# Two steps moved in the first attention stage of a decoder block: a weight copy on ScalarE, and the splitting of the next weights on GpSimd

## The chip, the core and the metric

The kernel runs on one core of one Trainium2 chip. Its engines each work through a queue of their own and meet only at semaphores: PE (TensorE, matmuls), DVE (VectorE), ACT (ScalarE), POOL (GpSimd) and SP (SyncE, which issues the DMAs). The metric is the device time of one execution in microseconds (us), and of several executions the median.

## The reference

The program is one decoder layer on 16 sequences of 128 tokens, model width 256, in float32. It has three parts, one after the other, each behind a layer norm and added to `x`:

```
x = x + attn(layernorm(x))            # stage A: windowed differential attention
x = x + xattn(layernorm(x), ctx_512)  # stage B: cross attention
x = x + ffn(layernorm(x))             # stage C: 16 experts, top 6, and a shared one
```

The change touches stage A alone. What it computes, for 16 query heads and 4 key heads of width 128:

```
q, k, v = x @ Wq, x @ Wk, x @ Wv ; q, k = rope(q), rope(k)
a1 = softmax(mask(q[:64] @ k[:64].T / 8)) ; a2 = softmax(mask(q[64:] @ k[64:].T / 8))
diff = relu(a1 - lam * a2) ; diff = diff / (sum(diff) + 1e-6)
out = (diff @ v) @ Wo
```

## The kernel before, in words

Stage A runs over 4 groups `g` of 4 query heads and, in each, over 16 units `u`, one for each sequence. `n = 16 g + u` counts them through. Units stand in chunks `c` of four; `j` is the place in the chunk. The work is pipelined over units. In unit `u` PE computes the scores of sequence `u`, transposes the normed weights of `u-2`, multiplies them by the values, and applies `Wo` to the output of `u-3`. Between these, in up to three slots for each unit, PE projects the q, k and v of the chunk that comes next: `A_SLOT` says which of the six items (k, q0, q1, q2, v, q3) stands in which slot.

The other engines serve this order:
- DVE (L1034 on) takes projections out of PSUM (`qab`, `ktmp`), computes `rec`, `ratio` and `rho` from the sums of the two softmaxes, the difference `a1 - lam a2` (L1072), the row maxima (L1126, L1127), the divisor `rden` (L1083), and adds `Wo`'s result to `x_sb` (L1088).
- ACT takes the transposes out of PSUM (`pt`), applies relu (L1478) and the exponentials (L1434, eight in a unit), copies the attention output (`oah`), and writes the mask into PSUM ahead of the next scores. ScalarE's copies all have line L1401.
- POOL multiplies the difference by `rden` (`a_norm`, L1665). PE's transposes in the same unit (L661, L663) wait for that, by `a_dn`. POOL also adds the two halves of the rotated key (`a_keys`, L1659).

Products are made exact enough by splitting operands into a high part (rounded to fp32r) and a low part (what the rounding left). For the weights of the next group, ACT makes the high part `wah` of a tile (`a_high`), once the tile's present content has been used for the last time, in units 8 to 11; POOL then makes the low part `wal` (`a_low`, L1653), which waits for `a_hi`. There are five such tiles for each group. For `Wo` ACT makes `woh` once in each group, in unit 3, DVE makes `wol` from it (L1131), and PE's `Wo` matmuls of unit 3 (L679) wait for `wol`.

Each engine's order is the order in which its function `a_unit` emits instructions, written out by hand. An engine that waits lets nothing behind it pass, PE's weight loads apart. Where loops over groups run (groups 1 and 2), the order is the same as in group 0.

Of the kernel before, what the change touches and what calls it, by code (L numbers as in the profile page):

```python
# [18 lines left out]
CB = 4  # L19
NC = B // CB  # L20
CW = CB * S
H, HG = 16, 4
# [77 lines left out]
def wait(eng, sem, value):  # L100

    if isinstance(value, int) and value <= 0:
        return
    eng.wait_ge(sem, value)


def decoder_kernel(nc, x, ctx_in, in_wqk, in_wv, in_wo, in_lam, in_taba, in_rawb, in_tabb, in_kvtab,
# [5 lines left out]
    def sem(name):  # L113
        return ctx.enter_context(nc.semaphore(name))

    def sb(stack, name, shape, dt=f32):
        return stack.enter_context(nc.sbuf_tensor(name, shape, dt))

    with ctx:
# [17 lines left out]
        wo = raw_w[:, 0:H * DM].rearrange("p (h d) -> p h d", d=DM)  # L137
# [23 lines left out]
        woh = sb(am, "woh", [128, HG, DM], f32r)  # L161
# [64 lines left out]
        def bank(n):  # L226
            return ps[:, n, :]

        def quads(ap):
            return ap.rearrange("p (h k) -> p h k", k=S)  # L230
# [12 lines left out]
        a_wvl, a_wld = sem("a_wv_loaded"), sem("a_weights_loaded")  # L243
# [10 lines left out]
        a_woh, a_wol, a_ol = sem("a_wo_high"), sem("a_wo_low"), sem("a_o_low")  # L254
        a_o, a_wo, a_y, a_nl = sem("a_o_high"), sem("a_out"), sem("a_x_added"), sem("a_nlam_ready")
# [29 lines left out]
        AN, AV = len(A_ITEMS), A_ITEMS.index("v")  # L285
        A_SLOT = {(0, 1): 0, (1, 0): 1, (1, 1): 2, (2, 1): 3, (3, 0): 4, (3, 1): 5}
# [13 lines left out]
        def a_part(first, final, drain):  # L300
            return "first" if first else "final" if final else "drain" if drain else ""

        def a_tile(item):

            return item - (item > AV)
# [8 lines left out]
        def a_split_tile(w, tile):  # L314
            return w[:, :, 128 * tile:128 * (tile + 1)].rearrange("p k (r n) -> p k r n", r=2)
# [82 lines left out]
        def a_blocks(ap):  # L398
            return [early(ap)[..., p, :] for p in range(XP)] + [late(ap)[..., p, :] for p in range(XP)]

        def by_head(ap):
            return ap.rearrange("p h (b q) -> p b h q", b=2)

        def by_block(ap):
            return ap.rearrange("p (b h q) -> p b h q", b=2, q=QH)
# [993 lines left out]
        def _(act):  # L1399
            def copy(dst, src):  # L1400
                return act.activation(dst, src, ACT.Copy)  # L1401

            def ln_take(m, kt, bk):

                tok = slice(CW * (m % NC), CW * (m % NC + 1))
                act.wait_ge(ln_tp, 2 * m + kt + 1)
                copy(xnf[:, kt, tok], bank(bk)).then_inc(ln_f, 1)
                copy(xnh[:, kt, tok], bank(bk)).then_inc(ln_h, 1)
# [7 lines left out]
            def a_high(g_to, tile):  # L1416

                act.wait_ge(a_raw, g_to * 16 + 16)
                copy(a_split_tile(wah, tile), a_raw_tile(tile)).then_inc(a_hi, 1)

            def a_take_v(g_to, c, turns=1):
                act.wait_ge(a_pj, (g_to * NC + c) * AN + (AV + 1))
                copy(quads(kva[:, c % 2, 2, :]), quads(bank(PJ - AV % turns))).then_inc(a_vf, 1)
# [14 lines left out]
            def a_unit(g, u, first=False, final=False, drain=False):  # L1438
                n, c, j = g * UN + u, u // CB, u % CB

                def slot(s):
                    item = A_SLOT.get((j, s))
                    if item is None or drain or (final and c == NC - 1):
                        pass
                    elif item == AV:
                        a_take_v(g + 1 if c == NC - 1 else g, (c + 1) % NC)
                    elif c == NC - 2 and not final:
                        act.wait_ge(a_pj, (g * NC + (NC - 1)) * AN + (item + 1))
                        a_high(g + 1, a_tile(item))
                    for what in A_EXTRA.get((a_part(first, final, drain), u, s), []):  # L1450
                        if what[0] == "ln":
                            ln_take(what[1], what[2], PJ)
                        elif what[0] == "prep":
                            b_take(0, 0, what, what[1], None, bank(PJ))
                        elif what[0] == "kt2":
                            r = what[1]
                            act.wait_ge(b_kvp, r + 1)
                            if r == 0:
                                act.wait_ge(a_sc, NG * UN - CB)
                            copy(kt2[:, CB * r:CB * (r + 1), :], quads(bank(PJ))).then_inc(b_kvc, 1)  # L1460
                if u == 3 and not drain:
                    if first:
                        act.wait_ge(a_wld, 32)
                    wait(act, a_wo, n - 3)
                    copy(woh[:, :, :], wo[:, bass.ds(g * HG, HG), :]).then_inc(a_woh, 1)
                slot(0)
                two = not (first and u < 2) and not (drain and u >= 2)
                if two:
                    act.wait_ge(a_tp, n - 1)
                    wait(act, a_pv, n - 3)  # L1470
                    copy(pt[:, u % 2, :, :], quads(bank(PTB))).then_inc(a_pt, 1)
                if not (first and u < 1) and not (drain and u >= 1):

                    act.wait_ge(a_df, n)
                    par = (u - 1) % 2
                    wait(act, a_dd, n - 2)
                    for h, e in enumerate(a_blocks(ea[:, par, 0, :])):
                        last = act.activation(e, e, ACT.Relu, accum_out=rsum[:, par, h:h + 1])  # L1478
                    last.then_inc(a_re, 1)
                if not drain:  # L1480
                    exps(n, u, 2, a_mx, a_ex, a_tp, lambda m, h: a_blocks(ea[:, u % 2, m, :])[h])
                slot(1)
                if two:
                    act.wait_ge(a_pv, n - 1)
                    wait(act, a_wo, n - 3)
                    copy(by_head(oah[:, (u - 2) % 2, :, :]), by_block(bank(OB))).then_inc(a_o, 1)
                if not drain and not (final and u >= UN - 2):
                    act.wait_ge(a_ex, n + 1)
                    copy(A_S[u % 2][:, :, 0:SW], maskb[:, :].unsqueeze(1).broadcast_to([128, 2, SW])).then_inc(a_mk, 1)
                if first and u == 1:  # L1490
                    for kt in range(KT):
                        ln_take(2, kt, OB + kt)
                slot(2)
# [74 lines left out]
            for u in range(UN):  # L1568
                a_unit(0, u, first=True)
# [62 lines left out]
        def _(pool):  # L1632
# [18 lines left out]
            def a_low(g_to, tile):  # L1651
                pool.wait_ge(a_hi, g_to * AW + (tile + 1))
                pool.tensor_tensor(a_split_tile(wal, tile), a_raw_tile(tile), a_split_tile(wah, tile).bitcast(f32),  # L1653
                                   ALU.subtract).then_inc(a_lo, 1)
# [20 lines left out]
            def a_unit(g, u, first=False, final=False, drain=False):  # L1675
                n, c, j = g * UN + u, u // CB, u % CB
                if not (first and u < 2):
                    a_norm(n - 2, u % 2)
                if first and u == 2:
                    ln_low(2)  # L1680
                if first and u == 7:
                    ln_low(3)
                if final and u == 8:
                    ln_rstd(4)
                if final and u == 12:
                    ln_low(4)
                if final and u == 13:
                    ln_rstd(5)
                if final and u == 15:
                    ln_low(5)  # L1690
                if drain and u == 0:
                    ln_rstd(6)
                if drain:
                    return
                if final and c >= NC - 2:
                    if u == UN - 2 * CB:
                        a_keys(g, NC - 1)
                    return
                if j == 0:
                    a_keys(g + 1 if c == NC - 1 else g, (c + 1) % NC)  # L1700
                if 0 < u - CB * (NC - 2) <= CB:
                    for s in range(2):
                        item = A_SLOT.get(((u - 1) % CB, s), AV)
                        if item != AV:
                            a_low(g + 1, a_tile(item))

            def c_low(g_to, t):
                pool.wait_ge(c_hi, g_to * TG + (t + 1))
# [59 lines left out]
            for u in range(UN + 1):  # L1768
                n = (NG - 1) * UN + u - 1
# [35 lines left out]
            for g in range(1, CG):  # L1805
                for k in range(NC * TG):
                    c, t = k // TG, k % TG
# [122 lines left out]
```

## Time and profile before

| | |
|---|---|
| median of 3 runs | 1346.95 us (1345.06 to 1347.26) |
| the profiled execution's own time | 1345.06 us |
| its span, first to last instruction | 1343.3 us |
| PE busy | 94% of the span |
| mean granted TensorE clock | 0.993 of full speed |

The span is what the engines worked in; 1.8 us of the execution lie around it. PE means matmuls, PEld their weight loads, which overlap them. A row of a timeline gives start, duration, engine, line, operation, output and inputs; `x2` behind it says that two like instructions were merged, and the square bracket says how long the engine had been idle and whose event ended that. Instructions of one engine overlap by about 0.1 us, since the next starts while the last writes its end.

### The profile page before, as it was taken

The numbers are of one execution on the slowest core, as the hardware profiler recorded it, in microseconds if no ns is written. First come the engines' busy times: TensorE is split into PE (matmuls) and PEld (weight loads), VectorE is DVE, ScalarE is ACT, GpSimd is POOL, SyncE is SP. The second block draws the span as 40 slices with busy tenths as digits, with TensorE's granted clock in tenths as the row PEclk, the third lists the DMA queues.
The fourth block names the chain that finished last, engine by engine and source line by source line (L and its number), as shares of the span: only waits on it lengthen the run. The fifth ranks groups of instructions, "written<-read, shape, count | busy, mean of one in ns | idle before, by whom it ended". The sixth has DMA issues, their size and how long they took to land.

```text
span 1343.3 us, 27486 instructions
## 1 busy us (share of the span) xinstructions
PE 1269.2 (94%) x9712; PEld 989.2 (74%) x9712; DVE 843.1 (63%) x1986; ACT 715.6 (53%) x2746; POOL 470.9 (35%) x467
## 2 busy tenths in 40 slices
PE   5799999999999788999999999989899999999998
PEld 4578888888887565666666666557788888888887
DVE  6788888888888676666656656765453333433333
ACT  2788888889887553444444444465232332423322
POOL 3122113112212134544544534541053353533532
PEclk9999999999999899999999999999999999999999
DMA  6011001100102101002002001000325342254230
GB/s 221 16 25 49 18 17 25 49 17 17 31 19 92 35 1 76 1 1 76 1 1 75 1 1 60 1 1 1 107 58 142 74 120 56 39 137 78 56 93 31
DMA packets 29810, 64.54 MB, mean 48 GB/s; under 512 B 6912, under 2 KB 12160, under 8 KB 28416
## 3 DMA queue, kind: packets, MB, share of 16 engines
q1 hardware_dynamic: 29696, 63.05, 17.6%
q8 instruction: 67, 1.10, 0.3%
q14 instruction: 47, 0.39, 0.1%
HBM read 52.42 MB, written 2.23 MB: 41 GB/s over the span
## 4 chain that ended last, share of the span: by engine, by line
PE 74%; DVE 10%; ACT 7%; issue 4%; POOL 2%; DMA 2%; SPq 1%; DVEq 0%; POOLq 0%; ACTq 0%
PE ps L531 31%; PE ps L923 9%; PE ps L647 5%; PE ps L716 4%; PE ps L679 4%; PE ps L820 4%; ACT ea L1434 3%; PE ps L810 3%; PE ps L792 3%; PE ps L800 2%; PE ps L670 2%; PE ps L586 2%; DMA cw<-comb_d 2%; ACT ea L1478 1%; DVE xnt L991 1%
## 5 line engine op out<-in xcount | busy, mean ns | idle before, releaser
L1798 POOL TENSOR_TENSOR sg<-sg,cw 128x512 f32<-128x512 f32 x88 | 113.5, 1290 | 260.1 <-ACT sg L1597 253.1
L1375 DVE TENSOR_TENSOR hh<-ps,sg 128x512 f32<-128x512 f32 x100 | 69.2, 692 | 178.6 <-POOL sg L1798 162.0
L1401 ACT ACTIVATE hhh<-hh 128x512 fp32r<-128x512 f32 x100 | 63.2, 632 | 214.7 <-DVE hh L1375 214.7
L1401 ACT ACTIVATE pt<-ps 128x512 f32<-128x512 f32 x128 | 76.9, 600 | 179.3 <-PE ps L800 122.6
L1434 ACT ACTIVATE ea<-ps,negmax 128x64 f32<-128x64 f32 (+1 forms) x512 | 164.6, 341 | 6.0 <-DVE negmax L1127 6.0
L531 PE MATMUL ps<-xnh,wch 128*128 128x512 f32 x400 | 157.0, 393 | 0.7 <-ACT pt L1401 0.7
L1174 DVE TENSOR_TENSOR qcs<-ps,tabb 128x512 f32<-128x512 f32 x192 | 123.6, 686 | 53.4 <-PE ps L531 53.1
L531 PE MATMUL ps<-xnl,wch 128*128 128x512 f32 x400 | 156.9, 392 | 0.0
L531 PE MATMUL ps<-xnh,wcl 128*128 128x512 f32 x400 | 155.6, 389 | 0.0
L1665 POOL TENSOR_TENSOR ea<-ea,rden 128x128 f32<-128x128 f32 (+1 forms) x128 | 62.1, 506 | 256.2 <-DVE rden L1083 256.2
L1672 POOL TENSOR_TENSOR eb<-eb,rsum 128x512 f32<-128x512 f32 x64 | 66.9, 1045 | 160.3 <-DVE rsum L1218 160.3
L923 PE MATMUL ps<-wch,hhh 128*128 128x256 f32 x400 | 115.9, 290 | 4.7 <-DVE hhl L1377 2.4
L1377 DVE TENSOR_TENSOR hhl<-hh,hhh 128x512 fp32r<-128x512 f32 x100 | 75.5, 755 | 69.8 <-ACT hhh L1401 69.8
L923 PE MATMUL ps<-wch,hhl 128*128 128x256 f32 x400 | 113.6, 284 | 0.0
L923 PE MATMUL ps<-wcl,hhh 128*128 128x256 f32 x400 | 113.6, 284 | 0.0
L1434 ACT ACTIVATION_READ_ACCUMULATOR ea<-ps,negmax 128x1 f32 x512 | 107.1, 209 | 0.0
L1434 ACT ACTIVATE eb<-ps,negmax 128x128 f32<-128x128 f32 x256 | 90.5, 368 | 29.4 <-DVE negmax L1212 29.1
L1088 DVE TENSOR_TENSOR x_sb<-ps,x_sb 128x256 f32<-128x256 f32 x128 | 54.1, 423 | 82.1 <-PE ps L820 58.4
L647 PEld LDWEIGHTS ps<-kva,qab 128*64 128x64 f32 x2048 | 93.2, 139 | 13.1 <-issue 7.9
L647 PE MATMUL ps<-kva,qab 128*64 128x128 f32 (+1 forms) x2048 | 102.4, 254 | 0.0
L679 PE MATMUL ps<-woh,oah 128*128 128x256 f32 x256 | 97.6, 381 | 0.7 <-DVE oal L1118 0.7
L1597 ACT ACTIVATE sg<-ps 128x512 f32<-128x512 f32 x100 | 59.9, 599 | 71.5 <-PE ps L531 70.6
(153 smaller groups left out, 3349.6 us busy)
## 6 DMA issues: line engine op xcount, KB each, us to landing
raw_w<-in_rawb_dram SPq DMA_DIRECT2D x4, 2432.0 KB, 9.0
kva<-ktmp SPq DMA_DIRECT2D x64, 128.0 KB, 2.4
cw<-comb_d SPq DMA_DIRECT2D x32, 256.0 KB, 5.0
raw_w<-in_rawc_dram SPq DMA_DIRECT2D x4, 1920.0 KB, 8.0
cw<-comb_d SPq DMA_DIRECT2D x16, 224.0 KB, 4.3
raw_a<-in_wqk_dram SPq DMA_DIRECT2D x4, 768.0 KB, 5.4
cw<-comb_d SPq DMA_DIRECT2D x16, 192.0 KB, 6.0
cw<-comb_d SPq DMA_DIRECT2D x16, 160.0 KB, 5.5
```

Source lines behind the costliest of these rows:

```text
L531: last = pe.matmul(out_ap, w, m, start=n == 0, stop=n == len(steps) - 1)
L647: last = pe.matmul(to[rows, h // 2, :], qab[:, c % 2, m, h, S * j + at:S * j + at + QH], kva[:, c % 2, m, S * j:S * j + keys], start=False ...
L679: last = pe.matmul(ps[:, YB, 0:DM], o_[:, (u - 3) % 2, h, :], w_[:, h, :], start=h == 0 and i == 0, stop=h == HG - 1 and i == 2)
L923: last = pe.matmul(ps[:, j // 2, DM * (j % 2):DM * (j % 2 + 1)], h_[:, par, S * j:S * (j + 1)], w_[:, t, 2 * KT * 128:RC_T], start=begin a ...
L1174: last = dve.tensor_tensor(quads(qcs[:, t, m, :]), quads(bk), bcast(tabb[:, b_table(t), m, :]), ALU.mult)
L1375: dve.tensor_tensor(hh[:, par, :], bank(C_U[par]), sg[:, par, :], ALU.mult).then_inc(c_h, 1)
L1377: dve.tensor_tensor(hhl[:, par, :], hh[:, par, :], hhh[:, par, :].bitcast(f32), ALU.subtract)\
L1401: return act.activation(dst, src, ACT.Copy)
L1434: last = act.activation(dst(m, h), src, ACT.Exp, bias=negmax[:, par, i:i + 1], accum_out=sums[:, par, i:i + 1])
L1665: last = pool.tensor_tensor(part, part, rden[:, par, XP * i:XP * (i + 1)].unsqueeze(2) .broadcast_to([128, XP, (QH, S)[i]]), ALU.mult)
L1672: pool.tensor_tensor(src[:, par, :, :], src[:, par, :, :], rec[:, par, :].unsqueeze(2).broadcast_to([128, HG, S]), ALU.mult).then_inc(done, 1)
L1798: pool.tensor_tensor(sg[:, par, :], sg[:, par, :], cw[:, c % 2, t, :], ALU.mult).then_inc(c_hs, 1)
```

## The change

On ACT, the copy of `Wo`'s high part (`woh`) in unit 3 of each group moves from the unit's beginning to behind the first slot and the copy `pt`. On POOL, the low parts of the next group's weights move one unit earlier: the tiles that ACT rounds in the slots of unit `u` are taken at the end of POOL's unit `u`, and no longer at the end of its unit `u+1`.

```
@@ ACT, a_unit
-                if u == 3 and not drain:
-                    if first:
-                        act.wait_ge(a_wld, 32)
-                    wait(act, a_wo, n - 3)
-                    copy(woh[:, :, :], wo[:, bass.ds(g * HG, HG), :]).then_inc(a_woh, 1)
                 slot(0)
                 if two:
                     act.wait_ge(a_tp, n - 1)
                     wait(act, a_pv, n - 3)
                     copy(pt[:, u % 2, :, :], quads(bank(PTB))).then_inc(a_pt, 1)
+                if u == 3 and not drain:
+                    if first:
+                        act.wait_ge(a_wld, 32)
+                    wait(act, a_wo, n - 3)
+                    copy(woh[:, :, :], wo[:, bass.ds(g * HG, HG), :]).then_inc(a_woh, 1)
@@ POOL, a_unit
-                if 0 < u - CB * (NC - 2) <= CB:
+                if c == NC - 2:
                     for s in range(2):
-                        item = A_SLOT.get(((u - 1) % CB, s), AV)
-                        if item != AV:
-                            a_low(g + 1, a_tile(item))
+                        if (j, s) in A_SLOT and A_SLOT[j, s] != AV:
+                            a_low(g + 1, a_tile(A_SLOT[j, s]))
```

On POOL, in groups 1 and 2, this stood in a row before, from the norm of unit 9 to the two low parts at the end of unit 10 (`ISA` and `REGISTER_ALU` set up addresses):

```order
L1665 TENSOR_TENSOR ea<-ea,rden 128x128 [waits a_norm_ready]
L1665 TENSOR_TENSOR ea<-ea,rden 128x256
L1652 ISA
L1653 TENSOR_TENSOR wal<-raw_a,wah 128x2x128 [waits a_w_high]
L1663 REGISTER_ALU
L1665 TENSOR_TENSOR ea<-ea,rden 128x128 [waits a_norm_ready]
L1665 TENSOR_TENSOR ea<-ea,rden 128x256
L1652 REGISTER_ALU
L1653 TENSOR_TENSOR wal<-raw_a,wah 128x2x128 [waits a_w_high]
L1652 REGISTER_ALU
L1653 TENSOR_TENSOR wal<-raw_a,wah 128x2x128 [waits a_w_high]
```

And this stands there now, from the low part at the end of unit 8 to the norm of unit 10:

```order
L1652 ISA
L1653 TENSOR_TENSOR wal<-raw_a,wah 128x2x128 [waits a_w_high]
L1663 REGISTER_ALU
L1665 TENSOR_TENSOR ea<-ea,rden 128x128 [waits a_norm_ready]
L1665 TENSOR_TENSOR ea<-ea,rden 128x256
L1652 REGISTER_ALU
L1653 TENSOR_TENSOR wal<-raw_a,wah 128x2x128 [waits a_w_high]
L1652 REGISTER_ALU
L1653 TENSOR_TENSOR wal<-raw_a,wah 128x2x128 [waits a_w_high]
L1663 REGISTER_ALU
L1665 TENSOR_TENSOR ea<-ea,rden 128x128 [waits a_norm_ready]
L1665 TENSOR_TENSOR ea<-ea,rden 128x256
```

Each norm of units 9 to 12 now stands behind low parts that wait for `a_w_high`, which ACT signals in the slots of the unit just before.

On ACT, unit 3 of groups 1 and 2, from the copy of the attention output of unit 2 to the relu of unit 3 (`kva` is the take of the v projection in the first slot):

```order
 L1401 ACTIVATE oah<-ps 128x2x4x64 [waits a_out,a_pv]
 L1401 ACTIVATE ps<-maskb 128x2x384 [waits a_exp]
+L1422 ISA
+L1401 ACTIVATE kva<-ps 128x512 [waits a_projected]
+L1401 ACTIVATE pt<-ps 128x512 [waits a_pv,a_transposed]
 L1401 ISA [waits a_out]
 L1401 ACTIVATE woh<-raw_w 128x1024
-L1422 ISA
-L1401 ACTIVATE kva<-ps 128x512 [waits a_projected]
-L1401 ACTIVATE pt<-ps 128x512 [waits a_pv,a_transposed]
 L1478 ACTIVATE ea,rsum<-ea 128x64 [waits a_denominator,a_difference]
```

`woh` passes `kva` and `pt` and now stands directly ahead of the relu. The orders of PE, DVE and SP are the same as before.

## Rows read from the trace of the kernel before

**Rows 1.** Page, part 1: busy us (share of the span) and instructions of each engine.

```profile
PE 1269.2 (94%) x9712; PEld 989.2 (74%) x9712; DVE 843.1 (63%) x1986; ACT 715.6 (53%) x2746; POOL 470.9 (35%) x467
```

**Rows 2.** Windows, group 1: length, busy us (instructions) by engine, PEclk, DMA share, GB/s.

```profile
157.70:264.40 106.70, 105.78 (x987) 87.85 (x985) 88.98 (x253) 91.81 (x442) 23.99 (x41) 1.00 0.12 29
```

**Rows 3.** Waits, 50 to 480 us: who waited for whom: us, times, longest.

```profile
PEld ps L531 <- DVE ktmp L1024: 3.7, 12, 0.5
...
PEld ps L661 <- POOL ea L1665: 3.5, 2, 2.3
```

**Rows 4.** Timeline, POOL, group 1, units 9 to 12.

```profile
204.74 0.97 POOL L1665 TENSOR_TENSOR ea<-ea,rden 128x128 f32<-128x128 f32 x2
...
210.52 0.97 POOL L1665 TENSOR_TENSOR ea<-ea,rden 128x128 f32<-128x128 f32 x2 [4.13 <-DVE rden L1083]
211.45 1.46 POOL L1653 TENSOR_TENSOR wal<-raw_a,wah 128x256 fp32r<-128x256 f32 x2
...
218.60 0.73 POOL L1653 TENSOR_TENSOR wal<-raw_a,wah 128x256 fp32r<-128x256 f32 x1 [0.69 <-ACT wah L1401]
223.80 0.97 POOL L1665 TENSOR_TENSOR ea<-ea,rden 128x128 f32<-128x128 f32 x2 [4.48 <-DVE rden L1083]
```

**Rows 5.** Timeline, ACT, group 1, units 9 to 11.

```profile
211.67 0.44 ACT L1401 ACTIVATE wah<-raw_a 128x256 fp32r<-128x256 f32 x1
...
213.19 0.63 ACT L1401 ACTIVATE pt<-ps 128x512 f32<-128x512 f32 x1
...
218.08 0.44 ACT L1401 ACTIVATE wah<-raw_a 128x256 fp32r<-128x256 f32 x1
...
224.85 0.45 ACT L1401 ACTIVATE wah<-raw_a 128x256 fp32r<-128x256 f32 x1
```

**Rows 6.** Timeline, PE, group 1: transposes of units 9, 10 and 12, first projection of 13.

```profile
206.54 0.41 PE L661 MATMUL ps<-idf,ea 128*64 128x128 f32 x2
...
212.27 0.41 PE L661 MATMUL ps<-idf,ea 128*64 128x128 f32 x2
...
225.81 0.41 PE L661 MATMUL ps<-idf,ea 128*64 128x128 f32 x2
...
230.41 0.50 PE L531 MATMUL ps<-xnh,wah 128*128 128x512 f32 x1 [0.30 <-DVE ktmp L1024]
```

**Rows 7.** Timeline, DVE, group 1, units 9, 10 and 12.

```profile
206.37 0.15 DVE L1066 TENSOR_TENSOR rho<-ratio,a_gap 128x4 f32<-128x4 f32 x1
...
212.05 0.16 DVE L1062 TENSOR_TENSOR ratio<-rec,sums 128x4 f32<-128x4 f32 x1
212.25 0.68 DVE L1066 TENSOR_TENSOR rho<-ratio,a_gap 128x4 f32<-128x4 f32 x1
...
213.46 0.99 DVE L1072 SCALAR_TENSOR_TENSOR ea<-ea,rho 128x64 f32<-128x64 f32 x4
...
228.27 0.68 DVE L1022 TENSOR_TENSOR ktmp<-ps,taba 128x512 f32<-128x512 f32 x1
```

**Rows 8.** Timeline, all engines, unit 3 of group 1.

```profile
165.90 1.08 ACT L1401 ACTIVATE woh<-raw_w 128x1024 fp32r x1
...
167.52 0.19 PEld L531 LDWEIGHTS ps<-xnh,wah 128*128 128x128 f32 x1 [0.27 <-ACT kva L1401]
...
167.53 0.60 ACT L1401 ACTIVATE pt<-ps 128x512 f32<-128x512 f32 x1
...
167.93 1.21 DVE L1131 TENSOR_TENSOR wol<-raw_w,woh 128x1024 fp32r<-128x1024 f32 x1
...
169.45 0.19 PEld L679 LDWEIGHTS ps<-woh,oah 128*128 128x128 f32 x1 [0.24 <-DVE wol L1131]
```

**Rows 9.** Windows, group 3, columns as in rows 2.

```profile
420.00:424.00 4.00, 2.24 (x11) 1.79 (x12) 3.64 (x11) 1.57 (x10) 1.71 (x3) 1.00 0.47 108
...
448.00:452.00 4.00, 1.39 (x8) 1.19 (x7) 1.40 (x4) 3.69 (x17) 0.00 (x0) 0.92 0.15 29
452.00:456.00 4.00, 3.29 (x35) 2.72 (x34) 3.86 (x17) 0.55 (x2) 0.69 (x2) 0.66 0.03 6
```

## The prediction

> **What bounds the kernel now.** I read the page's first part for the busiest engine, windows for where it is busiest, the waits for what stops it there, and then the timelines of the two places that the change touches. PE is busy for 94% of the span [rows 1]; in group 1 of stage A it is busy for 105.78 of 106.70 us at full clock [rows 2]. So there is under 1 us of air on PE in 107 us, and a wait put before PE in these units is paid nearly whole. ACT (91.81) and DVE (88.98) are close behind [rows 2], so they cannot make up much either. In the whole stage PE waits for POOL's norm twice, 3.5 us in all, and twelve times, 3.7 us in all, for the take of k [rows 3]; the second of these is the one place where a late PE gets something back. The groups 0, 1 and 2 repeat each other to 0.01 us in units 8 to 12, so I work one through and multiply.
>
> **The POOL edit, group 1.** Nothing is added; five low parts of 0.73 us each (1.46 for two, rows 4) and their waits move ahead of norms for which PE waits. POOL lets nothing pass, so behind each waiting low part stands the norm of the next unit, and behind that PE's transposes.
>
> Unit 8's low part stands between the key sum and the norm of unit 9. Its high part is ready, so it costs its 0.73: the norm, 204.74 to 205.71 before, ends at 206.44, and PE takes it at 206.54 [rows 4, 6]. Hidden, with 0.1 us left.
>
> Unit 9's second low part needs the high part that ACT makes only behind the eight exponentials of unit 9, at 211.67 to 212.11 [rows 5]. Handing over from ACT to POOL takes 0.08 us (218.08 + 0.44 to 218.60, rows 4, 5). So: 212.19 start, 212.92 end, norm of unit 10 (0.97) to 213.89; before it ended at 211.49 [rows 4]. PE wants it at 212.27 [rows 6]. PE is 1.65 us late.
>
> What moves with PE: in unit 10, ACT's `pt` (213.19, rows 5) needs PE's transposes and gets late, so the high part of that unit (218.08) comes about 0.6 us later. Its low part and the norm of unit 11 end near 220.5, and PE, 1.65 us late, comes for it after that: no second price there. At the v projection, which follows, PE gets 0.2 us back, since it had waited there for DVE. By unit 11 PE and ACT are both 1.45 us late.
>
> Unit 11's high part is then at 224.85 + 1.45; add 0.45 for itself, 0.08, the low part 0.73 and the norm 0.97: 228.53. PE, 1.45 late, wants it at 227.26 (225.81 in rows 6). The distance is 1.27 us, and it does not depend on how late both are. PE is now 2.7 us late.
>
> Then PE's take back: k is taken by DVE from 228.27, when PE had given it some 0.4 us before, and PE waited 0.30 us for that at 230.41 [rows 6, 7]. DVE is now released by PE and not by its own work, so 0.4 of the 2.7 us vanish. Remaining: 2.3 us for each group. From there all engines follow PE, and nothing is ahead that would wait for a fixed time; no group is the only one with slack.
>
> **A collision that adds to it.** While two low parts run (211.45 to 212.91, rows 4), DVE's little `rho` takes 0.68 us where `ratio` before it took 0.16 [rows 7]; it ends with the second low part. So a DVE operation with two inputs in SBUF stands still beside a POOL operation. After the change low parts and norms stand back to back just where DVE works on `rho` and the difference: the first low part at the end of POOL's unit 9 begins at 206.4, when `rho` of unit 9 is due (206.37), and could hold it for 0.55 us; ACT's exponentials and the high part at 211.67 follow this. The norm of unit 10 then runs beside the difference at 213.46, which waits up to 0.4 us. The first of these delays goes onto PE in full, the second is hidden behind `pt`. So a group costs between 2.3 and 2.9 us; I take 2.5, near the lower, because `rho` comes within 0.1 us of the low part's start and may win. Three groups (the last has no next weights): 7.5 us.
>
> The Trainium skill, SBUF — State Buffer, section "Who interferes with whom", states the same as a lock: a DVE instruction with two SBUF inputs and a GpSimd instruction that reads SBUF exclude each other for the whole instruction, whoever comes first. By this rule alone a group would cost 2.9 us rather than 2.3; the row of `rho` agrees (0.68 against 0.16).
>
> **The ACT edit, group 1.** Before, `woh` (1.08 us, at 165.90) stands ahead of `kva` and `pt`. `kva` now starts at 165.90 and PE's wait of 0.27 us for it goes [rows 8]. `pt` gains nothing: it starts at 167.53 because PE's transposes end then. `woh` follows at 168.03 and ends at 169.11. DVE's `wol` (1.21 us), at 167.93 before, starts at 169.15 and ends at 170.36; PE's `Wo` matmuls, at 169.45 before and already released by `wol`, start at 170.4 [rows 8]: +0.95 us. The gain of 0.27 lies ahead of this wait and is lost in it. Relu and exponentials start 0.95 later too, so ACT and DVE are as late as PE and nobody catches up. The same steps in the other groups give 0.8, 0.8 and 1.0. Together 3.5 us. If DVE hid `wol` entirely the edit would be worth -0.27 a group, -1 us; if the stall were the whole `woh` plus hand-overs, 1.2 a group, +5 us.
>
> **Sum.** 7.5 + 3.5 = 11.0 us. The profiled execution took 1345.06 us (span 1343.3 and 1.8 around it), which gives 1356.1; that execution was the fastest of the three, and against the median of 1346.95 it is 1358.0 us. DMAs don't enter: the weights' next load waits for the low parts and now starts some 3 us sooner, for a use 60 us later.
>
> **The rivals.**
> - *More collisions.* Each of the late low parts and norms catches a `rho` or a difference in its path, in units 9 to 12, and the order of arrival falls to POOL each time: 2.9 + 2 x 0.4 = 3.7 a group, 11 in three; with 3.5 to 5 for ACT, 1361 to 1363. For it: the row of `rho`. Against: most of the held work lies behind `pt`, which waits for PE.
> - *Only one edit is felt.* If the exponentials and the high parts kept ahead of PE, the norms would come in time and 3.5 us remain: 1350.5. Against: the high part ends at 212.11 and two POOL operations of 1.7 us stand between it and 212.27. Or `wol` is hidden and only 7 remain: 1354.
> - *Faster.* The held `rho` of units 10 and 11 lies in the chain to the exponentials, 0.52 us each; if the low parts move away from it, that is 3.1 us in three groups, and with `kva` earlier another 1.1: 1342.7. It decides at whether unit 10's norm is ready by 212.27; by rows 5 it isn't, by 1.65 us, and the moved low part starts at 212.19, on top of `rho` again.
> - *The clock.* PE's new idle stretches are 1.3 to 2.2 us. With 1.8 of 4 us idle at 420 us the clock stayed at 1.00; with 2.6 of 4 idle at 448 us it fell, to a mean of 0.66 in the next 4 us, so partly to the lower level of 1.2 GHz [rows 9]. Should it fall after each of six stalls, for about 4 us each, PE does 2 us less work each time: +12, 1370. The Trainium skill, TensorE: Matmul & The Clock Gate, section "HAM oscillation — how this bites in real kernels", warns of exactly this, idle gaps between bursts that return PE to half clock. The gaps here are shorter than the ones after which rows show it.
>
> **How the numbers follow.** Chances: the forecast (1354 to 1360.5) 0.62; more collisions (to 1363) 0.13; one edit felt alone (1350 to 1354) 0.12; clock 0.04; nothing to be seen 0.05; faster 0.04. The range 1350.5 to 1363 leaves out about 2 in 10, and holds both bounds of each term. What a measurement tells from no change is about 0.2%, 2.7 us: above 1349.6 is slower. That gives slower 0.91, same 0.05, faster 0.04.
>
> **What would show it.** In the changed profile: PE's transposes (L661) wait for POOL (L1665) six more times, about 1.7 and 1.3 us in each of three groups, some 9 us in all, at units 10 and 12; POOL waits for ACT's `wah` before low parts, about 5 us at a time; PE's `Wo` matmuls (L679) of unit 3 wait for `wol`, four times about 1 us; the wait of `L531` for `kva` is gone, and that for `ktmp` at unit 13 is near zero. Group 1 has grown by 3.3 to 3.9 us, group 3 by 1. Stages B and C are unchanged in length. I am wrong if the waits for POOL stay at two, or if group 1 has grown by less than 2 us.

## The result, and the profile after

The changed kernel takes 1358.93 us (median of 4 runs, 1356.94 to 1359.82), against 1346.19 us for the kernel before on the same chip: a ratio of 1.0104, 95% interval 1.0088 to 1.0119, or 12.7 us more. 1358.0 had been forecast. These four are the ones that stand beside runs of the kernel before; all ten executions of the changed kernel on record lie between 1356.94 and 1362.59 us, with a median of 1360.5. The profiled one took 1362.26 us, with a span of 1360.4, and is thus one of the longer ones; 17.1 us of span are to be explained in it, 4 more than the medians differ by.

The page after, part 1, and the stretch of group 1, cut at the same events as [rows 2]; columns as there:

```profile
PE 1276.8 (94%) x9712; PEld 993.5 (73%) x9712; DVE 847.4 (62%) x1986; ACT 715.7 (53%) x2746; POOL 470.8 (35%) x467
```

```profile
163.55:275.50 111.95, 107.27 (x987) 88.58 (x985) 90.38 (x253) 91.92 (x442) 23.92 (x41) 0.98 0.11 28
```

The columns are length, then busy us (instructions) of PE, PEld, DVE, ACT and POOL, the granted clock (PEclk), DMA share and GB/s. The same 987 matmuls take 111.95 us and not 106.70. PE is now idle for 4.7 us of this time and not for 0.9; it is also busy 1.5 us longer for the same work, and the clock column says 0.98: a second cost beside the waits.

What PE waited for in the kernel after, 50 to 496 us (who waited for whom: us, times, longest), against [rows 3]:

```profile
PEld ps L661 <- POOL ea L1665: 14.4, 8, 2.3
...
PEld ps L679 <- DVE wol L1131: 6.1, 4, 1.6
...
PEld ps L531 <- DVE ktmp L1024: 2.8, 12, 0.5
```

Six waits for POOL's norm are new, two were there, both in group 3. The wait for `wol` is new in this size (1.5 to 1.6 us each, 0.24 in [rows 8]), and that for `ktmp` has shrunk.

The timeline of PE at the transposes of units 9, 10, 11 and 12 of group 1, after (compare [rows 6]):

```profile
213.16 0.41 PE L661 MATMUL ps<-idf,ea 128*64 128x128 f32 x2
...
221.10 0.41 PE L661 MATMUL ps<-idf,ea 128*64 128x128 f32 x2 [2.17 <-POOL ea L1665]
...
230.22 0.41 PE L661 MATMUL ps<-idf,ea 128*64 128x128 f32 x2
...
237.21 0.41 PE L661 MATMUL ps<-idf,ea 128*64 128x128 f32 x2 [1.21 <-POOL ea L1665]
```

And POOL there, where low parts (`wal`) wait and norms (`ea`) stand behind them (compare [rows 4]):

```profile
212.06 0.97 POOL L1665 TENSOR_TENSOR ea<-ea,rden 128x128 f32<-128x128 f32 x2
212.99 0.72 POOL L1653 TENSOR_TENSOR wal<-raw_a,wah 128x256 fp32r<-128x256 f32 x1
219.40 0.72 POOL L1653 TENSOR_TENSOR wal<-raw_a,wah 128x256 fp32r<-128x256 f32 x1 [5.69 <-ACT wah L1401]
220.08 0.97 POOL L1665 TENSOR_TENSOR ea<-ea,rden 128x128 f32<-128x128 f32 x2
...
235.50 0.73 POOL L1653 TENSOR_TENSOR wal<-raw_a,wah 128x256 fp32r<-128x256 f32 x1 [7.46 <-ACT wah L1401]
236.19 0.96 POOL L1665 TENSOR_TENSOR ea<-ea,rden 128x128 f32<-128x128 f32 x2
```

POOL sits idle for 5.7 and 7.5 us with the norm standing behind the low part that waits; the norm ends at 221.05 and PE goes on at 221.10.

DVE's small operation `rho` in unit 9, beside the low part at 212.99 (before it took 0.15, [rows 7]), and in unit 10:

```profile
212.99 0.74 DVE L1066 TENSOR_TENSOR rho<-ratio,a_gap 128x4 f32<-128x4 f32 x1
...
219.46 0.68 DVE L1066 TENSOR_TENSOR rho<-ratio,a_gap 128x4 f32<-128x4 f32 x1
```

Unit 3 of group 1, all engines, after (compare [rows 8]):

```profile
171.75 0.63 ACT L1401 ACTIVATE kva<-ps 128x512 f32<-128x512 f32 x1
...
173.40 0.60 ACT L1401 ACTIVATE pt<-ps 128x512 f32<-128x512 f32 x1 [1.01 <-PE ps L663]
...
173.89 1.05 ACT L1401 ACTIVATE woh<-raw_w 128x1024 fp32r x1
...
175.09 1.22 DVE L1131 TENSOR_TENSOR wol<-raw_w,woh 128x1024 fp32r<-128x1024 f32 x1 [1.21 <-ACT woh L1401]
...
176.36 0.19 PEld L679 LDWEIGHTS ps<-woh,oah 128*128 128x128 f32 x1 [1.60 <-DVE wol L1131]
```

ACT stands idle for 1.01 us ahead of `pt`, while it waits for PE's transposes, and does `woh` afterwards. Before, `woh` stood ahead of `kva` and used up this time.

Since PE's transposes stand once in each unit, the start of L661 in both timelines gives the whole account. How much later it starts after than before, in us:

| | group 0 | group 1 | group 2 | group 3 |
|---|---|---|---|---|
| unit 3 | 0.56 | 5.87 | 11.08 | 14.46 |
| unit 4 | 1.48 | 6.59 | 11.65 | 15.11 |
| unit 9 | 1.51 | 6.62 | 11.67 | 15.20 |
| unit 10 | 3.70 | 8.83 | 13.89 | 16.81 |
| unit 11 | 4.96 | 10.12 | 13.56 | 16.76 |
| unit 12 | 6.24 | 11.40 | 14.83 | 16.75 |
| unit 13 | 5.83 | 11.09 | 14.52 | 16.75 |

From unit 3 to 4 of the four groups PE loses 0.92 + 0.72 + 0.57 + 0.65 = 2.9 us: the ACT edit. From unit 9 to 13 of group 2 it loses 2.22 - 0.33 + 1.27 - 0.31 = 2.85 us: the POOL edit. Groups 0 and 1 have the same steps but one: from unit 10 to 11 they lose 1.26 and 1.29 where group 2 gains 0.33. And in group 3, where nothing was changed at that place, 1.6 us come in from unit 9 to 10.

The granted clock tells why. PE in group 1 after, behind the stall of unit 10, where matmuls of one shape grow from 0.39 to 0.63 us:

```profile
222.03 0.39 PE L531 MATMUL ps<-xnh,wal 128*128 128x512 f32 x1
222.26 0.55 PE L531 MATMUL ps<-xnh,wah 128*128 128x512 f32 x1
222.61 0.63 PE L531 MATMUL ps<-xnl,wah 128*128 128x512 f32 x1
```

and the windows around it, beside those of the same place in group 2:

```profile
220.00:224.00 4.00, 2.90 (x11) 2.27 (x12) 3.08 (x9) 2.75 (x15) 1.05 (x3) 0.79 0.01 2
224.00:228.00 4.00, 4.00 (x25) 3.16 (x24) 2.15 (x7) 3.48 (x16) 1.63 (x3) 0.78 0.02 4
...
332.00:336.00 4.00, 2.95 (x15) 2.21 (x15) 3.63 (x10) 2.75 (x15) 1.00 (x3) 1.00 0.00 0
336.00:340.00 4.00, 4.00 (x48) 3.88 (x48) 3.02 (x10) 3.95 (x16) 1.66 (x3) 1.00 0.02 4
```

In groups 0 and 1 the clock fell to the lower of its two levels (1.2 GHz of 2.4) for a stretch behind a stall of 2.14 and 2.17 us; in group 2 it stayed up behind one of 2.15. A fall costs 1.29 + 0.33 = 1.6 us. The account of this execution: ACT 2.9, POOL 3 x 2.85 = 8.5, two falls 3.1, a fall in group 3 1.6, and 0.6 by which PE is late already in unit 3 of group 0. That makes 16.7 us, and the table ends at 16.75. The 0.6 are about 1 us from the start of stage A, ahead of any changed instruction (the second profile of the kernel before, below, has 0.9 there), less some 0.4 that the earlier `kva` gives back. So the ACT edit costs 2.9 us at the places of the table, and about 2.5 with these 0.4. The last 0.4 of the 17.1 us arise in stage C, where nothing was changed and the clock fell as before.

### The profile page after: what moved, and what is told of

Read it like the earlier page. It is cut to its first block, busy times and chain, and to the rows that moved or that the text cites. A ratio compares the mean times of both kernels' runs of the same rounds, so it can differ in the third digit from the quotient of the medians.

```text
span 1360.4 us, 27486 instructions
## 1 busy us (share of the span) xinstructions
PE 1276.8 (94%) x9712; PEld 993.5 (73%) x9712; DVE 847.4 (62%) x1986; ACT 715.7 (53%) x2746; POOL 470.8 (35%) x467
## 3 DMA queue, kind: packets, MB, share of 16 engines
q1 hardware_dynamic: 29696, 63.05, 17.1%
## 4 chain that ended last, share of the span: by engine, by line
PE 68%; issue 12%; DVE 8%; ACT 5%; POOL 4%; DMA 2%; SPq 1%; POOLq 0%; DVEq 0%; ACTq 0%
PE ps L531 29%; PE ps L923 9%; PE ps L716 4%; PE ps L820 4%; PE ps L647 4%; PE ps L679 3%; PE ps L810 3%; PE ps L792 3%; PE ps L800 2%; POOL ea L1665 2%; PE ps L670 2%; ACT ea L1434 2%; DMA cw<-comb_d 1%; PE ps L586 1%; DVE xnt L991 1%
## 5 line engine op out<-in xcount | busy, mean ns | idle before, releaser
L531 PE MATMUL ps<-xnh,wch 128*128 128x512 f32 x400 | 157.0, 393 | 0.7 <-ACT pt L1401 0.7
L531 PE MATMUL ps<-xnl,wch 128*128 128x512 f32 x400 | 156.9, 392 | 0.0
L531 PE MATMUL ps<-xnh,wcl 128*128 128x512 f32 x400 | 155.6, 389 | 0.0
L1665 POOL TENSOR_TENSOR ea<-ea,rden 128x128 f32<-128x128 f32 (+1 forms) x128 | 62.1, 506 | 225.5 <-DVE rden L1083 225.5
```

The source lines that it names most:

```text
L531: last = pe.matmul(out_ap, w, m, start=n == 0, stop=n == len(steps) - 1)
L1665: last = pool.tensor_tensor(part, part, rden[:, par, XP * i:XP * (i + 1)].unsqueeze(2) .broadcast_to([128, XP, (QH, S)[i]]), ALU.mult)
```

## The experiments

Times against the kernel before: chip A for the first four (before: 1347.28 us, 11 runs), chip B for the next four (1346.23 us, 27 runs); the last two are single runs on a third chip, beside one of the kernel before (1348.00 us). In brackets stand the ratio of the times and its 95% interval; 0.001 of it is 1.35 us.

**The POOL edit alone.** ACT as before.

```
                 if c == NC - 2:          # POOL, a_unit; instead of 0 < u - CB * (NC - 2) <= CB
                     for s in range(2):
                         if (j, s) in A_SLOT and A_SLOT[j, s] != AV:
                             a_low(g + 1, a_tile(A_SLOT[j, s]))
```

> The POOL edit alone, ACT as before. Theory: the norm behind the waiting low part costs PE 2.2 us in unit 10 and 1.25 us in unit 12 of groups 0, 1 and 2, of which 0.35 comes back in unit 13 and 0.3 at the v projection: 2.85 us a group, 8.5 us in all where the clock holds, and up to 1.6 us more for each group in which the clock falls behind the stall of unit 10. So +8.5 to +13 us, about 1356. Rival: the two edits hurt each other (ACT late in unit 3, POOL late in unit 10), and this one alone costs less than 6 us.

Measured: 1357.33 us, +10.0 (ratio 1.0070, 1.0056 to 1.0084). The waits of L661 for POOL are 2.18, 2.14 and 2.14 us in unit 10 and 1.22 in each unit 12; L661 slips by 2.86 us from unit 9 to 13 in groups 1 and 2, and by 4.40 in group 0, where the clock fell. The rival, under 6 us, is ruled out: the POOL edit doesn't need the ACT edit.

**The ACT edit alone.** POOL as before.

```
                 slot(0)                   # ACT, a_unit
                 if two:
                     ...
                     copy(pt[:, u % 2, :, :], quads(bank(PTB))).then_inc(a_pt, 1)
+                if u == 3 and not drain:
+                    ...
+                    copy(woh[:, :, :], wo[:, bass.ds(g * HG, HG), :]).then_inc(a_woh, 1)
```

The same lines ahead of `slot(0)` are gone.

> The ACT edit alone, POOL as before. Theory: PE waits about 1 us for wol in unit 3 of each of four groups and is spared 0.25 to 0.4 us for kva: +2.9 us in all, about 1349. Rival: the late low parts of the other edit are what makes ACT's delay felt; alone, the time stays within 1 us of before.

Measured: 1351.64 us, +4.4 (1.0031, 1.0019 to 1.0042). Its steps from unit 3 to 4 are 0.91, 0.72, 0.57 and 0.64 us, 2.8 in all, so 1.5 us more than the stalls are left. The interval of the time, 2.6 to 5.7 us, holds the 2.8, so that it is not sure that this rest exists; see the second profile below.

**The POOL edit without the meeting of the first low part and `rho`.**

```
+                    if j == 1:            # in the POOL edit's branch
+                        pool.wait_ge(a_df, n)
```

> The POOL edit, with one more wait: the low parts at the end of POOL's unit 9 wait for DVE's difference in that unit, so that the first of them doesn't run beside rho. Theory (a held rho makes ACT's exponentials and the high part later): PE's stall in unit 10 falls from 2.2 to 1.65 us, the time by 0.5 us a group, 1.5 us less than with the POOL edit alone; if a shorter stall also spares the clock, up to 5 us less. Rival (the wait for the high part alone makes the stall, rho doesn't count): stall and time as with the POOL edit alone.

Measured: 1353.92 us, +6.6 (1.0041, 1.0027 to 1.0054), 3.4 us below the POOL edit alone. `rho` in unit 9 of group 1, and PE's stall there:

```profile
208.25 0.15 DVE L1066 TENSOR_TENSOR rho<-ratio,a_gap 128x4 f32<-128x4 f32 x1
```

```profile
215.78 0.41 PE L661 MATMUL ps<-idf,ea 128*64 128x128 f32 x2 [1.58 <-POOL ea L1665]
```

One more wait on POOL, and PE is 0.57 us less late, three times: 1.7 us. No fall of the clock stood behind any of the three stalls of 1.6 us, where the POOL edit alone had one in its profile; a fall costs 1.6 us, about the size of the rest.

**The POOL edit with PE's stalls filled.** The fill also writes over zeros that are kept in that bank, so the attention output of this version is not the layer's.

```
                 if two:                   # PE, a_unit
+                    wait(pe, a_pt, n - 2)
+                    if u in (10, 12) and not final and not drain:
+                        for _ in range(7 if u == 10 else 4):
+                            pe.matmul(bank(PTB), woh[:, 0, 0:128], xnh[:, 0, 0:512], start=True, stop=True)
                     pe.wait_ge(a_dn, n - 1)
-                    wait(pe, a_pt, n - 2)
```

> The POOL edit, and PE fills its stalls: seven matmuls of 512 columns ahead of the transposes of unit 10, four ahead of those of unit 12, in groups 0 to 2, into the bank that the transposes then overwrite. Theory (the idle of 2.2 us lets the clock fall): the clock stays at full speed in groups 0 to 2 in every execution, the times of single executions stand closer together, and the median is some 2 to 3 us below that of the POOL edit alone, +8.5 us against before. Rival (the clock falls by chance, not from the stall): the same spread and the same mean clock as with the POOL edit alone.

Measured: 1355.18 us, +7.9 (1.0056, 1.0042 to 1.0069), single executions between 1354.49 and 1356.06, where the POOL edit alone had 1356.15 to 1358.37. The kernel has three more lines ahead, so L664 and L1668 are the L661 and L1665 of the others. Group 1, unit 10:

```profile
214.95 1.89 PE L657 MATMUL ps<-xnh,woh 128*128 128x512 f32 x7
217.18 0.41 PE L664 MATMUL ps<-idf,ea 128*64 128x128 f32 x2 [0.34 <-POOL ea L1668]
```

The transposes start as late as in the POOL edit alone; only PE is busy meanwhile. The clock didn't fall in groups 0 to 2, and L661 slips by 2.75, 2.85 and 2.87 us in them. So the stalls cost 8.5 us at full clock, and PE's idleness in them adds to it by way of the clock: the mean granted clock is 0.988 in all five executions of the POOL edit alone, and 0.992 in four of the five here.

**Only the first slots' tile early.**

```
                 if 0 < u - CB * (NC - 2) <= CB:   # tiles of second slots: one unit behind, as before
-                    for s in range(2):
-                        ...
+                    item = A_SLOT.get(((u - 1) % CB, 1), AV)
+                    if item != AV:
+                        a_low(g + 1, a_tile(item))
+                if c == NC - 2:                   # tiles of first slots: in the same unit
+                    if (j, 0) in A_SLOT and A_SLOT[j, 0] != AV:
+                        a_low(g + 1, a_tile(A_SLOT[j, 0]))
```

> Of the POOL edit only the tile whose high part ACT makes in a first slot (item 1, slot 0 of unit 9) is taken one unit early; the tiles of second slots stay one unit behind, as before. Theory (the cost comes from low parts whose high part stands behind the eight exponentials): no wait of PE's transposes for POOL in groups 0 to 2, time within 1 us of before. Rival (more POOL work in unit 9 delays the norms and rho as such): +0.5 us a group or more, 1.5 to 3 us in all.

Measured: 1348.25 us, +2.0 (1.0010, 1.0001 to 1.0019). The rival was right: PE never waits for POOL's norm in groups 0 to 2, and yet L661 slips by 0.6 us in each group. POOL and `rho` in units 9 and 10 of group 1:

```profile
207.34 1.42 POOL L1653 TENSOR_TENSOR wal<-raw_a,wah 128x256 fp32r<-128x256 f32 x2
```

```profile
208.04 0.74 DVE L1066 TENSOR_TENSOR rho<-ratio,a_gap 128x4 f32<-128x4 f32 x1
...
214.51 0.70 DVE L1066 TENSOR_TENSOR rho<-ratio,a_gap 128x4 f32<-128x4 f32 x1
```

The second of two low parts in a row now holds `rho` in unit 9; ACT's relu and exponentials start late, and the one low part left for unit 10 meets the equally late `rho` again. The late `rho` reaches PE by way of `pt` (a wait of L670 for `pt`, 0.20 us) and of the take before v (0.23 us); before, PE waited at neither place.

**`woh` between the first slot and `pt`.** POOL as before.

```
                 slot(0)                   # ACT, a_unit
+                if u == 3 and not drain:
+                    ...
+                    copy(woh[:, :, :], wo[:, bass.ds(g * HG, HG), :]).then_inc(a_woh, 1)
                 two = not (first and u < 2) and not (drain and u >= 2)
```

The same lines ahead of `slot(0)` are gone here too.

> POOL as before; the copy woh of unit 3 stands between the first slot (the take of v) and the copy pt, where ACT waits for PE's transposes anyway. Theory: kva comes early enough and wol is not late, so the ACT edit's gain stays and its loss goes: PE's wait for kva (0.25 to 0.4 us, four times) is gone, the wait for wol stays as before: -1.4 us, about 0.1%. Rival (ACT is the bound in unit 3, so any place of woh costs the same): no gain, or +1 us through a late pt.

Measured: 1344.78 us, -1.45 (0.9990, 0.9981 to 0.9999). ACT, PE's weight loads and DVE in unit 3 of group 1:

```profile
166.20 0.63 ACT L1401 ACTIVATE kva<-ps 128x512 f32<-128x512 f32 x1
166.68 1.10 ACT L1401 ACTIVATE woh<-raw_w 128x1024 fp32r x1
...
167.55 0.19 PEld L531 LDWEIGHTS ps<-xnh,wah 128*128 128x128 f32 x1
...
167.86 0.60 ACT L1401 ACTIVATE pt<-ps 128x512 f32<-128x512 f32 x1
...
168.25 1.22 DVE L1131 TENSOR_TENSOR wol<-raw_w,woh 128x1024 fp32r<-128x1024 f32 x1
...
169.52 0.19 PEld L679 LDWEIGHTS ps<-woh,oah 128*128 128x128 f32 x1 [0.29 <-DVE wol L1131]
```

`woh` fills the time in which ACT waits for PE's transposes; PE waits 0.29 us for `wol`, where it waited 0.24 before, and the wait of L531 for `kva` is gone.

**The same, and low parts kept away from `rho` and the difference.**

```
                 if 0 < u - CB * (NC - 2) <= CB:   # POOL, a_unit, tiles as before
+                    pool.wait_ge(a_df, n)
                     for s in range(2):
```

> As the version with woh between the first slot and pt, and POOL's low parts, one unit behind as before, also wait for DVE's difference of their unit, so that none runs beside rho or the difference. Theory (a rho held for 0.5 us in units 10 and 11 is felt by DVE's later takes, for which PE waits 0.2 us at v and 0.3 us at ktmp): a further 0.5 us a group at most, -1.4 to -3 us against before. Rival: those 0.5 us are hidden, and the time is that of the version before it.

Measured: 1343.70 us, -2.5 (0.9981, 0.9972 to 0.9990), the fastest version. `rho` takes 0.16 us in units 9 to 11, and L661 gains a further 0.20 to 0.23 us in each of three groups, from unit 10 to 11. Less than the 0.5 us by which each `rho` is freed: the rest was hidden. That is 0.65 us in three groups; the two medians differ by 1.1, and their intervals overlap.

**Both edits, once more.**

> Both edits, the changed kernel once more, on the chip of its neighbours. Theory: +2.9 us (ACT) and +8.5 us (POOL) of stalls at full clock, and up to 1.5 us for each group in which the clock falls behind the stall of unit 10: +12 to +14 us. In the profile the clock falls in some of groups 0 to 2 behind the 2.2 us stall, and not in all. Rival (the clock's falls in groups 0 to 2 were one execution's chance): none in this profile.

Measured: 1361.09 us, +14.9 (1.0112, 1.0096 to 1.0127; 4 runs). Stalls of 2.14, 2.17 and 2.17 us in unit 10. The windows behind those of groups 0, 1 and 2:

```profile
108.00:112.00 4.00, 3.70 (x11) 3.00 (x12) 2.08 (x7) 2.60 (x16) 0.25 (x1) 0.57 0.00 0
...
222.00:226.00 4.00, 4.00 (x21) 2.86 (x20) 1.81 (x5) 4.00 (x20) 0.97 (x2) 0.71 0.00 0
...
334.00:338.00 4.00, 4.00 (x34) 3.59 (x34) 3.02 (x9) 4.00 (x20) 0.97 (x2) 1.00 0.02 4
```

Again groups 0 and 1, and not 2. The time lies above the +12 to +14 us that were expected; its interval (12.9 to 17.1 us) overlaps with theirs and with that of the first measurement (11.8 to 16.0).

**The kernel before, a second profile.**

> The kernel before once more, for a second profile. Theory: PE's idle stretches and waits repeat to 0.1 us, the clock stays at 1.00 in groups 0 to 2, and where it falls at the start and end of stage A differs from the first profile by one or two stretches. Rival (each kernel has its falls at fixed places): the falls stand where they stood.

Measured: 1348.24 us (1348.00 for the other run of it there), span 1346.4, against 1343.3 in the first profile. Group 3 behind the wait for POOL of 2.18 us, which both profiles have ([rows 9] for the first):

```profile
422.77 0.41 PE L661 MATMUL ps<-idf,ea 128*64 128x128 f32 x2 [2.18 <-POOL ea L1665]
```

```profile
424.00:428.00 4.00, 4.00 (x15) 2.75 (x14) 1.99 (x5) 4.00 (x27) 0.56 (x2) 0.64 0.99 281
```

L661 of the next unit is 1.6 us later than in the first profile, and at the start of stage A, where its clock falls more often (mean 0.72 from 36 to 40 us, against 1.00), it is 0.9 us late. Another 0.6 us arise in stage C, without a further fall. So the same program is 3.1 us longer in span, 2.5 of it where the clock differs, and the profile on which the prediction was worked out was a lucky one: it shows no fall behind the stall of group 3. In groups 0 to 2 the clock holds in both.

**The ACT edit alone, a second profile.**

> The ACT edit alone once more, for a second profile, since its time was 1.4 us more than its stalls. Theory (more half-clock stretches at the end of stage A, by chance of that execution): PE's waits in unit 3 repeat, 2.9 us in all, and the falls at the end of stage A are fewer than in its first profile, with a shorter span. Rival (the edit sets them): the same falls at the same places.

Measured: 1350.74 us. The rival was right. At the end of stage A both profiles of this version have a fall that neither profile of before has; the first and the second:

```profile
480.00:484.00 4.00, 4.00 (x43) 3.51 (x41) 3.18 (x9) 1.73 (x5) 1.34 (x1) 0.62 0.00 0
```

```profile
480.00:484.00 4.00, 4.00 (x39) 3.47 (x36) 3.41 (x11) 2.13 (x10) 1.34 (x1) 0.57 0.00 0
```

L661 slips by 0.98 and 0.92 us more from unit 14 of group 3 to the drain behind it, and another fall stands near 498 us (0.75 and 0.70), behind which PE is a further 1.6 us late. PE has idle stretches there in every version. Together this is 2.5 to 2.7 us against both profiles of before, more than the 1.5 us that the stalls don't explain. But both profiles of the two edits together, which hold the same ACT edit, lose less than 0.1 us at that place. So it is no cost of the moved copy as such, and why the clock falls there in this version stays open.

## Why the prediction was right, and what it had wrong

- *What bounds.* Right: PE has no air in groups 0 to 2, and a stall before it is paid. The filled version shows it for the POOL edit: 2.75 to 2.87 us a group at full clock.
- *The norm of unit 10.* The wait for the high part behind the exponentials was forecast to make PE 1.65 us late, and 2.2 with a held `rho`. Measured 1.58 without the meeting, 2.14 to 2.18 with it.
- *The norm of unit 12.* Forecast 1.27 late, however late both are; measured waits of 1.21 and 1.22 in every version that has it unfilled, and a slip of 1.27.
- *The take back.* Forecast 0.2 at v and 0.4 at k; measured 0.33 and 0.31 in groups where the clock held.
- *The collision.* Here the term was mis-sized: I took 2.5 us a group, between 2.3 and 2.9, since `rho` might win. It lost in every group of all four profiles that let the two meet (the rival of more collisions had said so), and a group costs 2.85: 8.5 us and not 7.5. The rule of the Trainium skill (SBUF — State Buffer, section "Who interferes with whom") gave 2.9, and the runs bear it out (2.85 a group, and 0.6 less with the meeting taken away).
- *The ACT edit.* The mechanism was right and the size too large. Forecast 3.5; PE slips 2.9, or about 2.5 with what `kva` gives back in group 0. `Wo`'s first matmuls start 1.04 us late in group 1 (169.45 before, 176.36 - 5.87 after), but the second weight load follows at once (176.47) and not after the 0.4 us that it takes without a stall: 0.3 us come back while PE stands. The timed cost of the edit alone, +4.4, is 1.5 us more than its stalls, within its interval.
- *The clock.* This step failed. I gave it 0.04, because "the gaps here are shorter than the ones after which rows show it". Behind stalls of 2.14 to 2.18 us in unit 10 it fell in 5 of 9 (both edits twice, POOL alone once), and behind the like wait in group 3 in 5 of 12 profiles; behind 1.58 us in none of 3 and behind 1.2 us in none of 12. That the row at 420 us, itself a stall of 2.2 us, showed no fall was a draw and not a bound. The price forecast for a fall, 2 us, was near: 1.6. The Trainium skill's warning of idle gaps (TensorE: Matmul & The Clock Gate, section "HAM oscillation — how this bites in real kernels") holds here for stalls of 2.2 us, in part of the cases; the waits in its own example are longer than these.
- *The signs.* The six new waits, the four for `wol` and the lost one for `kva` came as said. Group 1 grew by 5.2 us and not by 3.3 to 3.9, and group 3 by 2.2 and not by 1: each of them holds a fall of the clock of 1.6 us.

So the cost was forecast at 11.0 us and measured at 12.7 and, the second time, 14.9. Two errors cancel, 0.6 to 1.0 too much for ACT against 1.0 too little for the collisions. The clock was left out; by subtraction it is some 1 to 4 us, an estimate. That 1358.0 lies only 0.9 us from 1358.93 is in part luck: the forecast was counted from 1346.95 where the kernel before then took 1346.19, and the four executions compared are on the short side of the ten. And the chances given outside the range of 1350.5 to 1363 add up to 0.13, not to the 2 in 10 stated. What decides that it is groups 0 and 1 and not 2 whose clock falls stays open; the stalls are alike to 0.03 us.

The rival that ended faster had a true part: `woh` out of `kva`'s way and low parts out of `rho`'s are worth 1.45 and, together, 2.5 us, but `woh` has to stand ahead of `pt`, and the low parts have to start later, not sooner.

## What to carry to other kernels

Before moving work behind a wait, see whether the wait is time that the work could fill (`woh` ahead of `pt`: -1.45 us; behind it: +4.4). Work that nobody needs soon has no business ahead of work that someone waits for, least of all with a wait of its own: low parts that are needed some four units later held up two norms in each of three groups. And a single profile tells the clock's falls of one execution: a new stall as long as one behind which the clock fell in any profile should be priced with a fall.

## What the runs showed of the hardware

- The granted clock fell behind single stalls of 2.1 to 2.3 us in 10 of 21 cases, behind 1.6 us in none of 3 and behind 1.2 us in none of 12, in a stretch where PE was otherwise busy; a fall cost 1.6 us here.
- The same program differed by 3.1 us in span between two executions, 2.5 of it at places where the clock fell in one of them and not in the other.
- With matmuls in place of two idle stretches in each of three groups the clock held, and the time fell from 1357.33 to 1355.18 us.
- A DVE operation on 4 columns with two inputs in SBUF took 0.68 to 0.74 us beside a POOL operation of 0.73 and 0.15 without, and ended within 0.03 us of it; POOL's own duration didn't change (0.72 to 0.74 us with and without).
- Where `rho` came up just as POOL went over to its low part (208.04 in the version with the first slots' tile early, 212.99 in the changed kernel), the low part went first: it was so in all 12 groups of the four profiles with the POOL edit in which the two meet. Where a norm stood behind the low part, `rho` got in when the low part ended (219.46 to 220.14 beside 219.40 to 220.12).
